# Attention on a graph: the destination rows of 30 of 49 batches gathered during the merge before, kept in HBM and loaded by SyncE

## The reference, cut to what matters

```
def _transformer_conv(x, src, dst, edge_attr, wq, bq, wk, bk, wv, bv, we, ws, bs, n_nodes):
    q, k, v, e = x @ wq + bq, x @ wk + bk, x @ wv + bv, edge_attr @ we
    ke = k[src] + e
    score = sum(q[dst] * ke) / sqrt(64)
    a = exp(score - segment_max(score, dst)[dst])
    alpha = a / segment_sum(a, dst)[dst]
    out = segment_sum(alpha * (v[src] + e), dst)
    return out + x @ ws + bs
h1 = relu(conv1(relu(layernorm(x)))); h2 = relu(conv2(h1)); relu(concat(h1, h2) @ skip_w + skip_b)
```

## Time and profile before

| | us |
|---|---|
| median of 3 runs | 8765.82 (8748.99 to 8783.12) |
| span of the profiled execution, first to last instruction | 7386.2 |
| median less span | 1379.6 |
| relation messages (re) | 1969 to 2515 |
| merge rew | 2526 to 2867 |
| scores at1s | 2871 to 3956 |
| merge at1w | 3990 to 4332 |
| scores at2s | 4333 to 5349 |
| merge at2w | 5383 to 5725 |

### The profile page before, as it was taken

How to read it: one execution, slowest core, us unless ns; L and a number is a source line. 1 busy time by engine, 2 the same in 40 slices (tenths; PEclk the granted TensorE clock), 3 DMA queues, 4 the chain that set the end, 5 groups by cost and what they waited for, 6 DMA issues and landing times. The chain is left out here.

```text
span 7386.2 us, 101314 instructions
## 1 busy us (share of the span) xinstructions
PE 4675.6 (63%) x31722; PEld 4192.0 (57%) x31722; DVE 4503.1 (61%) x5720; ACT 1623.3 (22%) x2242; POOL 3795.4 (51%) x3348
## 2 busy tenths in 40 slices
PE   4665335760188785555555866666668774784797
PEld 2354334650177785555555866666568774674675
DVE  6998443222577786666667842232398894683457
ACT  0143112330143343222222421111134340000001
POOL 0198565563277403777771047777600006766766
PEclk9866668995599998766767987777789996997899
DMA  2298666656722374332333753334357883122009
GB/s 75 48 276 259 140 147 140 138 108 201 252 73 73 101 245 154 83 79 79 81 78 101 249 164 109 109 109 112 100 186 250 304 307 112 49 59 91 14 12 278
DMA packets 837873, 1024.59 MB, mean 139 GB/s; under 512 B 589119, under 2 KB 601812, under 8 KB 836380
## 3 DMA queue, kind: packets, MB, share of 16 engines
q1 hardware_dynamic: 534716, 742.63, 31.5%
q0 software_dynamic: 144256, 90.12, 8.3%
q10 hardware_dynamic: 158560, 187.31, 7.6%
HBM read 608.19 MB, written 417.84 MB: 139 GB/s over the span
## 5 line engine op out<-in xcount | busy, mean ns | idle before, releaser
L839 POOL DMA_INDIRECT gc_msgs<-t,src_rows x784 | 754.4, 962 | 1098.1 <-POOLq L146 804.2
L893 POOL DMA_INDIRECT acc<-de_sums,de_put x392 | 608.5, 1552 | 410.9 <-DMA acc<-de_sums,de_put 263.5
L1913 PEld LDWEIGHTS gc_ring<-gc_msgs,gc_hot 128*128 128x128 f32 x4736 | 628.4, 210 | 305.9 <-issue 298.1
L1913 PE MATMUL gc_ring<-gc_msgs,gc_hot 128*128 x4736 | 654.9, 297 | 230.4 <-SPq L1872 229.3
L839 POOL DMA_INDIRECT at2s_ends<-h,src_rows x392 | 369.9, 944 | 533.6 <-POOLq L146 414.4
L839 POOL DMA_INDIRECT at1s_ends<-x,src_rows x392 | 389.2, 993 | 490.5 <-POOLq L146 371.3
L1027 PE MATMUL de_ring<-de_win,de_pick 128*128 x2368 | 343.2, 305 | 272.7 <-DMA de_win<-t 272.7
L1027 PEld LDWEIGHTS de_ring<-de_win,de_pick 128*128 128x128 f32 x2368 | 322.9, 217 | 295.0 <-issue 289.1
L839 POOL DMA_INDIRECT at1s_ends<-x,dst_rows x392 | 419.0, 1069 | 119.5 <-issue 119.5
L839 POOL DMA_INDIRECT re_rows<-x,src_rows x392 | 406.5, 1037 | 125.1 <-issue 124.8
L1393 PE MATMUL re_psR<-w_rel,re_own 128*128 128x128 f32 x3136 | 398.6, 293 | 73.6 <-DVE re_own L1330 73.3
(11 more groups left out here) (471 smaller groups left out, 11359.4 us busy)
## 6 DMA issues: line engine op xcount, KB each, us to landing
rew_win<-x SPq DMA_DIRECT2D x74, 544.0 KB, 4.0
at1w_win<-g SPq DMA_DIRECT2D x74, 544.0 KB, 4.0
at2w_win<-g SPq DMA_DIRECT2D x74, 544.0 KB, 4.0
de_near<-same SPq DMA_DIRECT2D x74, 512.0 KB, 5.1
de_win<-t SPq DMA_DIRECT2D x74, 512.0 KB, 4.6
x<-rew_win SPq DMA_DIRECT2D x74, 512.0 KB, 2.9
h<-at1w_win SPq DMA_DIRECT2D x74, 512.0 KB, 2.9
h<-at2w_win SPq DMA_DIRECT2D x74, 512.0 KB, 2.9
```

The costliest lines, as they stand in the source:

```text
L839: nc.gpsimd.indirect_dma_start(buf[:, t * width:(t + 1) * width], None, table, bass.IndirectOffsetOnAxis(ap=rows[:, t:t + 1], axis=0)).the ...
L893: nc.gpsimd.indirect_dma_start(g.acc0[j % 2], bass.IndirectOffsetOnAxis(ap=put[:, j:j + 1], axis=0), sums[:, j * D:(j + 1) * D], None, com ...
L1913: done = nc.tensor.matmul(ring[:, bass.ds(to[n], SLOT)], hot[k][:, n, :], each_group(msgs[:, bass.ds(of[n], MID)], SLOT // MID), start=Fal ...
```

## The change

In the merges rew and at1w, GpSimd gathers the destination rows of batches 0 to 29 (EARLY = 30) of the following score stage from the table that the merge is writing, as soon as enough blocks have been stored: a new column of `places` holds, for each batch, how many blocks that is, and SyncE signals each landed block (`landed`). The rows go through three SBUF tiles into a table `near` in HBM, by a plain DMA of 262 KB a batch from GpSimd (`keep`). In the score stage GpSimd gathers only source rows for these batches, and SyncE loads the destination rows from `near`. SyncE also collects the arrival of gathers and loads into one semaphore (`arrive`), for which TensorE and VectorE wait. SyncE's stage order is written out and no loop any more. The tables x2 and h1 are filled with zeros once, in the degree stage and in the relation stage.

```
@@ -49,6 +49,7 @@
 QUARTERS = 4
+EARLY = 30
@@ -211,6 +212,7 @@
         g.passed = ctx.enter_context(nc.semaphore("passed"))
+        g.near_got, g.near_kept = ([ctx.enter_context(nc.semaphore(f"near_{n}{k}")) for k in range(3)] for n in ("got", "kept"))
@@ -226,6 +228,7 @@
         g.attr = table("attr", P * T, DE)
+        g.near = [table(f"near{k}", P, EARLY * B * D) for k in range(2)]
@@ -253,7 +256,7 @@
             g.opens = brief("opens", [P, 2, 3 * HALF], i32)
-            g.places = brief("places", [P, 4], i32)
+            g.places = brief("places", [P, 5], i32)
@@ -277,9 +280,9 @@
             attention_edges(nc, g, "at1", g.x2, True, ("q1", "k1", "v1", "e1"), ("bq1", "bk1", "bv1"),
-                            [("s1", "bs1", g.g1)], g.g1, g.h1)
+                            [("s1", "bs1", g.g1)], g.g1, g.h1, g.near[0], 1)
             attention_edges(nc, g, "at2", g.h1, False, ("q2", "k2", "v2", "e2"), ("bq2", "bk2", "bv2"),
-                            [("s2", "bs2", g.g2), ("skip_a", "bskip", g.skip)], g.g2, g.h2)
+                            [("s2", "bs2", g.g2), ("skip_a", "bskip", g.skip)], g.g2, g.h2, g.near[1], None)
@@ -347,13 +350,14 @@
         ahead, edge_bank, other_bank = (r.sb(n, [P, S]) for n in ("ahead", "edge_bank", "other_bank"))
-        need, ended, moved = (r.sb(n, [P, 1]) for n in ("need", "ended", "moved"))
+        need, ended, moved, begin = (r.sb(n, [P, 1]) for n in ("need", "ended", "moved", "begin"))
+        begun = r.sb("begun", [P, P])
...
-        cleared, loaded, weights, attrs, numbered, link_s, row_made, passed, turned, taken, stepped, path_made, path_put, path_in, ends_made, ends_turned, line_put = (
+        cleared, loaded, weights, attrs, numbered, link_s, row_made, passed, turned, taken, stepped, path_made, path_put, path_in, ends_made, ends_turned, line_put, begun_made, begun_summed = (
             r.sem(n) for n in ("cleared", "loaded", "weights", "attrs", "numbered", "link", "row_made", "passed", "turned", "taken", "stepped",
-                               "path_made", "path_put", "path_in", "ends_made", "ends_turned", "line_put"))
+                               "path_made", "path_put", "path_in", "ends_made", "ends_turned", "line_put", "begun_made", "begun_summed"))
@@ -476,6 +480,8 @@
                 link(v.tensor_tensor(node[:, :], at[:, :], edge[:, :], ALU.subtract))
+                link(v.tensor_scalar(begin[:, :], node[:, 0:1], float(P), None, ALU.mult))
+                v.tensor_scalar(begun[:, :], lasts, begin[:, :], None, ALU.is_ge).then_inc(begun_made, 1)
@@ -511,6 +517,8 @@
                 link(v.tensor_scalar(g.blocks[:, 1:2], need[:, :], 1.0, None, ALU.add))
+                dve.wait_ge(begun_summed, 1)
+                v.tensor_copy(g.places[:, 4:5], ps_row[1][:, 0:1])
@@ -536,6 +544,8 @@
                 nc.tensor.matmul(ps_row[0][:, P:2 * P], g.ones[:, :], diag[:, 1, :], start=True, stop=True).then_inc(ends_turned, 1)
+                pe.wait_ge(begun_made, 1)
+                nc.tensor.matmul(ps_row[1][:, 0:1], begun[0:BLOCKS, :], g.ones[0:BLOCKS, 0:1], start=True, stop=True).then_inc(begun_summed, 1)
@@ -646,7 +656,15 @@
         link_s = r.sem("link")
+        zeroed = r.sem("zeroed")
         with nc.Block() as block:
+            @block.sync
+            def _(sp):
+                def clear(b):
+                    sp.dma_start(chunk_of(g.x2, b.number), g.zeros[:, 0:J * D]).then_inc(zeroed, 16)
+                pipeline(sp, clear)
+                sp.wait_ge(zeroed, 16 * STEPS)
@@ -1105,7 +1123,7 @@
-def merge_rows(nc, g, name, msgs, base, to, alpha=None, counts=None):
+def merge_rows(nc, g, name, msgs, base, to, alpha=None, counts=None, near=None):
@@ -1119,6 +1137,11 @@
         stored = r.sem("stored")
+        landed = r.sem("landed")
+        if near is not None:
+            rows = [r.sb(f"rows{k}", [P, W]) for k in range(3)]
+            got, kept = g.near_got, g.near_kept
+            before = [near * len(range(k, EARLY, 3)) for k in range(3)]
@@ -1140,7 +1163,7 @@
                     if m >= 1:
-                        sp.wait_ge(stored, 16 * m)
+                        held(sp, stored, 16 * m, landed)
@@ -1153,7 +1176,26 @@
                 store(BLOCKS - 1)
-                sp.wait_ge(stored, 16 * BLOCKS)
+                held(sp, stored, 16 * BLOCKS, landed)
+            if near is not None:
+                @block.gpsimd
+                def _(pool):
+                    def keep(b):
+                        pool.wait_ge(got[b % 3], 16 * B * (before[b % 3] + b // 3 + 1))
+                        pool.dma_start(g.near[near][:, b * W:(b + 1) * W], rows[b % 3][:, :]).then_inc(kept[b % 3], 16)
+                    for b in range(EARLY):
+                        need = pool.value_load(g.places[2 * b + 1:2 * b + 2, 4:5], min_val=1, max_val=BLOCKS)
+                        held(pool, landed, need, g.passed)
+                        if b >= 3:
+                            held(pool, kept[b % 3], 16 * (before[b % 3] + b // 3), g.passed)
+                        gather(nc, rows[b % 3], to, g.dst_rows[:, b * B:(b + 1) * B], got[b % 3])
+                        if b >= 1:
+                            keep(b - 1)
+                    keep(EARLY - 1)
+                    for k in range(3):
+                        pool.wait_ge(kept[k], 16 * (before[k] + len(range(k, EARLY, 3))))
@@ -1252,7 +1294,7 @@
         relation_messages(nc, g, a, msgs)
-        merge_rows(nc, g, "rew", msgs, g.x1, g.x2, counts=g.dinv)
+        merge_rows(nc, g, "rew", msgs, g.x1, g.x2, counts=g.dinv, near=0)
@@ -1297,7 +1340,9 @@
                                  a["edge_type_8"][b.number * C:b.number * C + n].unsqueeze(0).to_broadcast([P, n])).then_inc(types_in[b.slot], 16)
+                    sp.dma_start(chunk_of(g.h1, b.number), g.zeros[:, 0:J * D]).then_inc(zeroed, 16)
                 written_out(load)
+                sp.wait_ge(zeroed, 16 * STEPS)
@@ -1402,18 +1447,18 @@
                 written_out(order=[(0, turn), (1, relate)], slots=4)
-def attention_edges(nc, g, name, nodes, normalise, weights, biases, dense, base, to):
+def attention_edges(nc, g, name, nodes, normalise, weights, biases, dense, base, to, near, near_next):
...
-        attention_scores(nc, g, name, nodes, normalise, weights, biases, dense, scores, values)
+        attention_scores(nc, g, name, nodes, normalise, weights, biases, dense, scores, values, near)
         segment_softmax(nc, g, name, scores)
-        merge_rows(nc, g, name + "w", values, base, to, scores)
-def attention_scores(nc, g, name, nodes, normalise, weights, biases, dense, scores, values):
+        merge_rows(nc, g, name + "w", values, base, to, scores, near=near_next)
+def attention_scores(nc, g, name, nodes, normalise, weights, biases, dense, scores, values, near):
@@ -1436,6 +1481,8 @@
         got, ea_in, stored = ([r.sem(f"{n}{k}") for k in range(SLOTS)] for n in ("got", "ea_in", "stored"))
+        near_in = [r.sem(f"near_in{k}") for k in range(2)]
+        arrived = r.sem("arrived")
@@ -1448,7 +1495,8 @@
                     gather(nc, ends[s][:, 0:W], nodes, columns(g.src_rows, b), got[s])
-                    gather(nc, ends[s][:, W:C], nodes, columns(g.dst_rows, b), got[s])
+                    if b.number >= EARLY:
+                        gather(nc, ends[s][:, W:C], nodes, columns(g.dst_rows, b), got[s])
@@ -1460,6 +1508,14 @@
                     sp.dma_start(xd[b.slot % 2][:, :], chunk_of(nodes, b.number)).then_inc(ea_in[b.slot], 16)
+                    if b.number < EARLY:
+                        sp.dma_start(ends[b.slot][:, W:C], near[:, b.number * W:(b.number + 1) * W]).then_inc(near_in[b.slot % 2], 16)
+                def arrive(b):
+                    if b.number < EARLY:
+                        sp.wait_ge(near_in[b.slot % 2], 16 * (b.number // 2 + 1))
+                    gathers = b.nth + len(range(EARLY + (b.slot - EARLY) % SLOTS, b.number + 1, SLOTS))
+                    held(sp, got[b.slot], 16 * B * gathers, arrived)
@@ -1469,10 +1525,10 @@
                     sp.sem_inc(o_free, 1)
-                pipeline(sp, order=[(0, load), (3, store), (4, landed)], slots=SLOTS)
+                written_out(order=[(0, load), (3, store), (4, landed), (0, arrive)], slots=SLOTS)
             def inputs_ready(eng, b):
-                eng.wait_ge(got[b.slot], 16 * 2 * B * b.nth)
+                eng.wait_ge(arrived, b.number + 1)
                 eng.wait_ge(ea_in[b.slot], 32 * b.nth)
             @block.tensor

```

2 lines of the change are left out of this document (1 added, 1 removed).

## The result

The changed kernel takes 8391.7 us (median of 4 runs, 8384.4 to 8397.1), the kernel before 8757.4 in the same series (4 runs, 8722.7 to 8783.1): a ratio of 0.957, 95% interval 0.954 to 0.960.

What follows compares the result with a forecast made beforehand. The prediction took both score stages to be bound by GpSimd's issue of gathers. Its terms, -208 - 127 + 142 + 132 + 10 + 1 = -50 us, gave 8716 us from a median of 8765.8, range 8500 to 8810.

Steps and rivals of the forecast that it cites:

- 1379.6 longer, outside the profiled instructions, and I leave that untouched: Whole kernel: median run 8765.8 us against a profiled span of 7386.2, the difference assumed outside the instructions and unchanged.
- Paces before: Score stages of the kernel before: 21.4 and 20.1 us a batch, both set by GpSimd's issue of gathers.
- Paces of early batches: Score stages, batches 0 to 29 with 8 gathers: the consumer's pace, 15.46 and 17.7 us a batch.
- The two terms: Score stages one and two: 208 and 127 us gained because batches 0 to 29 need 8 gathers, not 16.
- The merges: Two merges: hot builds hold GpSimd to two issues a block, the others follow alone; 142 and 132 us added.
- the variant that I weighed from the Trainium skill: Merges: plain stores that only write SBUF pass the hot build undelayed, so the 30 stores take 24 us away.
- Traffic and the longer blocks: Merges: kept batches of 262 KB may delay window loads; 10 us for both merges, 0 to 30.
- The rival of the long blocks: Merges: loads land later and blocks lengthen, deciding from 0.94 us a block; +50, 8816 us, chance 0.18.
- The rest: Zeroing x2 hidden in the degree stage, zeroing h1 0 to 5 us, SyncE's wait within rounding, setup 1 us.
- The rival of the slow score stages: Score stages: SyncE's loads, stores and waits in one order keep them off the consumer's pace; +28, 8794 us, chance 0.12.
- the hot build doesn't hold GpSimd: Merges: gathers run undisturbed beside the one-hot build, so merges cost 17 + 21 us; 8470 us, chance 0.18.
- The signs that I named for being wrong: Both merges together growing by under 200 us, or the two score stages shrinking by less than 280.

Runs made afterwards that it cites:

- rest: The changed kernel with all destination rows gathered in the score stages again and nothing gathered in the merges: 8820.1 us, ratio 1.0002 to the kernel before.
- one_input: The changed kernel with each merge's one-hot build comparing one operand with zero instead of two operands with each other: 8590.9 us, ratio 0.972 to the kernel before.

## Why the prediction was wrong

- **The step that failed**: "1379.6 longer, outside the profiled instructions, and I leave that untouched". It was inside them, in the stages where GpSimd gathers (score stages +204 and +384, convolutions +757, relation stage +88, together 1433; the two profiles are 1426 apart). The rows and runs above show TensorE held there in the convolutions and score stages, where GpSimd's waits for TensorE alone are 179.5 and 337.6 of the 204 and 384; in the relation stage its signals are late beside the gathers as well, but no run took the hold off there with a gain. The two score stages that the change works on had 588 us of it.
- **Paces before**: 21.4 and 20.1 us a batch, 25.7 and 28.0 in the second profile. "Both are bound by how fast GpSimd issues gathers" holds only for the execution that I read; in the timed ones GpSimd waits for TensorE.
- **Paces of early batches**: forecast 15.46 and 17.7; measured 15.5 and 17.1. Right: with 8 gathers a batch TensorE keeps up.
- **Late batches**: forecast 21.4 and 20.1; measured 24.6 and 25.7.
- **The two terms**: -208 was -306, -127 was -332. With 25.7 and 28.0 as the paces before, 29 early batches give 29 x 10.2 = 296 and 29 x 10.9 = 316, 19 late ones 19 x 1.1 = 21 and 19 x 2.3 = 44: 317 and 360, near what was measured. That fewer gathers bring a batch down to the consumer's pace was right; what a heavy batch costs, and which engine bounds it, was taken from the wrong execution. The forecast has -50 and the stages -417; 303 of the 367 us between them lie in this step.
- **The merges**: +142 and +132 forecast and 10 for traffic, +118 and +111 measured. The step was right in kind: 71 of the 73 gathers that started inside a hot build of merge one ended 0.8 us after it, and none was long in the tail. What I missed is that 2.6 issues fit a block in the mean, not 2 (190 until the last store, in 72 blocks). A block takes 4.65 us, so a third gather, due at h + 4.65, can start just ahead of the next build (I take it, no run parts this); and no store is held: the seven stores that start inside a build take 0.58 to 0.59 us. My block of 4.36 was 323 us over 74, but 74 builds have 73 steps between them: 4.43. (The stores are the variant that I weighed from the Trainium skill, SBUF — State Buffer, "Who interferes with whom", by which only a GpSimd instruction that reads SBUF is held; the stores' rows agree.)
- **Traffic and the longer blocks**: from first to last store merge one takes 338.5 us, 17 more, and merge two 330.6, 9 more, in part hidden behind the tail. The rival of the long blocks decides from 0.94 us a block; they lengthened by 0.22 (4.65 against 4.43).
- **The rest** (zeroing, SyncE's order and wait, setup): forecast near nothing, and rest shows 0.0002 of the time. (In stage two's pace the last start of the earlier trace rows is 5321.6 and not 5321.4; 20.14 stands.) The rival of the slow score stages falls with it.
- **Rivals**: "the hot build doesn't hold GpSimd" would have given 8470, nearer to the time than my forecast, and is false; one_input shows it. A time alone doesn't tell which mechanism holds. The signs that I named for being wrong (merges under +200, score stages under -280) watched one side only: at +229 and -638 neither spoke up.
- **Chances**: 0.52 for faster; the range left out what turned out to be the largest unknown, a sixth of the time that no view accounted for.

Left open: why one execution ran without the hold and all the others with it, though its gathers come as densely (1.25 to 1.29 us apart in the convolutions), and through what TensorE is held. No run here changed either.

## What to carry to other kernels

Compare the profiled execution's span with the timed runs before anything else is worked out from it: if they differ by more than a few per cent, the paces read from it are those of another execution, and the difference belongs to some stage. Where GpSimd streams indirect gathers beside matmuls, look at when TensorE's semaphores rise and not at its modelled ends; a short operation of GpSimd after each gather can be worth more than taking gathers away (a ratio of 0.920 by itself, against 0.957 for the change); both together, with every second batch relieved, did best here (0.865). Price a gather by the mean distance of two starts, not by the median: the one is 1.57, the other 1.44 in score stage one with rests, and two of the expectations above missed by it. An operation that blocks one engine may be what keeps another running, so measure before freeing it.

## What the runs showed of the hardware

- Indirect gathers issued every 1.25 to 1.33 us by GpSimd hold TensorE to one matmul in 0.71 us (one batch of a score stage) or 2.8 us (convolution) in every trace but one, and in that one they don't; VectorE and ScalarE are not slowed. With 0.33 us of memset between two, 70 blocks of 74 are done beside them in place of 5; with 0.22 us, 66 and 67.
- Plain DMAs of GpSimd, every 0.56 us, don't hold TensorE.
- A two-input VectorE comparison of 2.28 us makes a gather caught by it end 0.8 us behind it (71 of 73); plain stores started inside it take 0.58 to 0.59 us (7).
